# Cross-attention stage: turn of normed rows ahead of the first weighted sums, and four steps moved on ScalarE, GpSimd and VectorE

## The chip, the cores and the metric

The kernel runs on one NeuronCore of a Trainium2 chip. Its engines run unsynchronised, each with a queue of its own, and meet only at semaphores: TensorE (PE, with its weight loads shown apart as PEld), VectorE (DVE), ScalarE (ACT), GpSimd (POOL) and SyncE (SP), which here only issues DMAs. The metric is the device time of the whole program in microseconds, as the median of several runs.

## The reference

A decoder layer on 64 sequences of 64 tokens, width 256, all in float32: self-attention with 32 heads, cross-attention, and a mixture of 8 experts with one shared expert. The change touches only the stage of the middle one. Cut to what matters:

```python
x = x + attn(layernorm(x))                       # self-attention, 32 heads of 64, 8 KV heads, sinks, RoPE
x = x + xattn(layernorm(x), ctx, ctx)            # 8 heads that split the TOKENS: 8 tokens each, m = n = 256
x = x + ffn(layernorm(x))                        # top-1 of 8 experts, and a shared expert

def xattn(q, k, v):                              # b = 64, d = c = 64, m = n = 256
    qh, kh, vh = (a.reshape(b * 8, 8, 256) for a in (q, k, v))
    qk = einsum('bdm,bdn->bmn', qh, kh) / sqrt(8)
    sm = softmax(qk, axis=-1)
    return einsum('bmn,bcn->bcm', sm, vh).reshape(b, c, m)

def ffn(x):
    logits = x @ router_w.T                      # 8 experts
    # the best one, its sigmoid score scales the row that goes to it
```

## The kernel before, in words

Self-attention (`attention`) runs first and leaves, for each tile of 128 tokens (two sequences), the operands of the cross-attention in DRAM, stacked in 96 rows. Then `cross` runs over NT = 32 tiles with 16 heads each, and `experts` follows.

`cross` is a software pipeline in which each engine has its own `body(tile, one, two, three, four, five)`. In the body of `tile` the engine works on five tiles at once: `tile` itself (stage one), the one before it `w` (two), `v` two before it (three), `z` three before it (four) and `y` four before it (five). `tiles` peels the first 4 tiles, loops over 24 in steps of 4, and peels the rest. A body has STEPS = 8 steps r = 0 to 7. The order of the calls in a body is the order in the engine's queue, and a call that waits for a semaphore holds all that is behind it in that queue. Nothing but these written orders sets the schedule.

What each engine does for a body:

- TensorE, at every step: half of a pair of transposed score blocks (`turned_scores_x`, L1288, two matmuls each into one of two banks of bankXT, each may start when ScalarE's exp has read what stood there), four score matmuls for two heads (`scores_x`, L1276, into two of four banks of bankX), and the other half of the pair. From step 4 on the turned scores are those of `w`, up to step 3 those of `v`. The first turned scores of a tile, at step 4, wait for the rows 96 and 97 of stq, which carry the negated maxima (the shift of the softmax) and come by DMA. Beside these: `turn_max` at step 1 (turns the maxima of `w` into bankM), `results_x(v, 0)` at step 1 and `results_x(v, 1)` at step 5 (the weighted sums of `v`, 32 column-tiled instructions each, into bankN), `turn_norm` at step 2 (turns the normed rows of `y` into bankM), `logits` at step 3, `rank` behind the second sums at step 5, `turn_ctx` at step 7.
- VectorE: `max_x` (L1190) at every step, a reduction over the two heads that `scores_x` left; `invert(z)` at step 0 (reciprocal of the denominators, L1204), `normalise(y)` at step 1 (L1218), `choose(y)` at step 4, `place(y)` ahead of the maxima of step 6 (it waits for `rank`), `stats_of(z)` at step 7.
- ScalarE: two exps of 128 x 512 at every step (`exp_x`, L1143), and ahead of them `evac_ctx` at step 0, `evac_shift` (L1112) at 2, `evac_norm` (L1124) at 3, `exp_score` (L1129) at 5, `evac_sums` (copies bankN into nd, L1117) at 6, `scale_row` (L1136) at 7.
- GpSimd: `quotient(z)` (three operations, L1027, L1030, L1033), `weigh(y)` (1 / (1 + exp(-score)), L1046 to L1050), `send(y)` (the indirect DMA of the routed rows), `split_max(tile)`, `spread(z)`.
- SyncE, in this order: the inverses out (waits for `invert`), the shifts into stq (L956), the inverses in (L915), x2 out, the context and the stacked operands of the next tile (L898, L903), x1 in, the denominators (L976, L977, wait for `evac_sums`), the normed rows out.

Of the kernel before, what the change touches and what calls it, by code (L numbers as in the profile page):

```python
# [98 lines left out]
def need(eng, sem, value):  # L99

    if isinstance(value, int) and value <= 0:
        return
    eng.wait_ge(sem, value)
# [679 lines left out]
def cross(nc, A, G, NT, NRT):  # L783
# [6 lines left out]
    with ExitStack() as pb:  # L790
# [66 lines left out]
        def prev(tile, n):  # L857

            k = tile[1] - n
            return tile[0] + k // U, k % U  # L860

        def at(tile):
            return tile[0] * U + tile[1]

        def inside(tile):
            return not isinstance(at(tile), int)
# [121 lines left out]
        def _(pool):  # L988
# [54 lines left out]
            def weigh(y):  # L1043

                pool.wait_ge(c_fin, at(y) + 1)
                need(pool, s_xr3, at(y))  # L1046
                settle(y, 2)
                nc.gpsimd.tensor_scalar(score[:, 1:2], score[:, 0:1], 1.0, None, ALU.add).then_inc(g_sc, 1)
                pool.wait_ge(g_sc, at(y) + 1)
                nc.gpsimd.tensor_tensor(score[:, 2:3], score[:, 1:2], minus[:], ALU.pow).then_inc(s_esc, 1)  # L1050
# [19 lines left out]

            def body(tile, one, two, three, four, five):
                z, y = prev(tile, 3), prev(tile, 4)
                if four:
                    quotient(z)
                if five:
                    weigh(y)
                    send(y)
                if one:
                    split_max(tile)
                if four:  # L1080
                    spread(z)
                if not inside(tile) and 1 <= at(tile) < 4:
                    split_shared(at(tile) - 1)
# [13 lines left out]
        @block.scalar  # L1097
        def _(act):
            def evac_ctx(w):
                act.wait_ge(s_cTp, at(w) + 1)  # L1100
                need(act, s_xp, (at(w) - 1) * 2)
                if isinstance(at(w), int) and at(w) == 0:
                    act.wait_ge(s_zc, 2)
                nc.scalar.activation(cT[w[1] % 2][:, :, :, 0:XD],
                                     bM[:, 0, 0:D].rearrange("p (k h c) -> p k h c", k=2, c=XD),
                                     ACT.Copy).then_inc(s_cT, 1)

            def evac_shift(w):
                act.wait_ge(s_shp, at(w) + 1)
                r = prev(w, 2)  # L1110
                need(act, s_sh[r[1]], (r[0] + 1) * 32)
                nc.scalar.activation(sh[w[1] % 2][:], bM[0:32, 0, D:2 * D], ACT.Copy).then_inc(s_shv, 1)  # L1112

            def evac_sums(v):
                act.wait_ge(s_xp, (at(v) + 1) * 2)
                need(act, s_num, at(v) - 1)
                nc.scalar.activation(nd[v[1] % 2][:], bN[:, 0, :].rearrange("p (k m) -> p k m", k=2),  # L1117
                                     ACT.Copy).then_inc(s_nd, 1)

            def evac_norm(y):  # L1120
                act.wait_ge(s_f3p, at(y) + 1)
                o = prev(y, 1)
                need(act, s_fst[o[1] % 2], (pair(o) + 1) * 32)
                nc.scalar.activation(xn3T[:], bM[:, 0, 0:D].rearrange("p (k n) -> p k n", k=2),  # L1124
                                     ACT.Copy).then_inc(s_f3, 1)

            def exp_score(y):
                act.wait_ge(s_top, at(y) + 1)
                nc.scalar.activation(score[:, 0:1], top8[:, 0:1], ACT.Exp, scale=-1.0).then_inc(c_fin, 1)  # L1129

            def scale_row(y):

                yp = y[1] % 2
                act.wait_ge(s_esc, at(y) + 1)
                need(act, s_scat[yp], pair(y) * 16)
                nc.scalar.activation(xr[yp][:, 0:D], xn3[yp][:], ACT.Copy, scale=score[:, 2:3]).then_inc(s_xr3, 1)  # L1136

            def exp_x(w, q):
                head = at(w) * XH + q
                act.wait_ge(s_xst, head + 1)  # L1140
                if q % 8 == 0:
                    need(act, s_xp, at(w) * 2 + q // 8 - 1)
                nc.scalar.activation(xe[q][:].rearrange("p n m -> p (n m)"), bT[:, q % 2, :],  # L1143
                                     ACT.Exp).then_inc(s_xe, 1)

            def body(tile, one, two, three, four, five):
                w, v, z, y = prev(tile, 1), prev(tile, 2), prev(tile, 3), prev(tile, 4)
                for r in range(STEPS):
                    if three and r == 0:
                        evac_ctx(v)  # L1150
                    if two and r == 2:
                        evac_shift(w)
                    if five and r == 3:
                        evac_norm(y)
                    if five and r == 5:
                        exp_score(y)
                    if three and r == 6:
                        evac_sums(v)
                    if five and r == 7:
                        scale_row(y)  # L1160
                    if two and r >= LAG:
                        exp_x(w, 2 * (r - LAG))
                        exp_x(w, 2 * (r - LAG) + 1)
                    if three and r < LAG:
                        exp_x(v, 2 * (r + STEPS - LAG))
                        exp_x(v, 2 * (r + STEPS - LAG) + 1)

            def high_x(g):
                act.wait_ge(G.s_xin[g % 2], 16 * (g // 2 + 1))
                need(act, G.s_u, FF // P * (g - 1))  # L1170
                nc.scalar.activation(G.xsh[g % 2][:], G.xs[g % 2], ACT.Copy).then_inc(G.s_xs0, 1)

            def ahead_of(t):
                if t == NT + 1:
                    high_x(0)

            G.act = evac_norm, exp_score, scale_row, high_x
            tiles(act, body, ahead_of)

        @block.vector  # L1180
        def _(dve):
# [63 lines left out]
            def body(tile, one, two, three, four, five):  # L1245
                z, y = prev(tile, 3), prev(tile, 4)
                routing = Chain(dve, c_rt, 4, at(y))
                for r in range(STEPS):
                    if five and r == 6:
                        place(y, routing)  # L1250
                    if one:
                        max_x(tile, r)
                    if four and r == 0:
                        invert(z)
                    if five and r == 1:
                        normalise(y)
                    if five and r == 4:
                        choose(y, routing)
                    if four and r == 7:
                        stats_of(z)  # L1260
# [9 lines left out]
        def _(pe):  # L1270
# [54 lines left out]
            def turn_norm(y, two):  # L1325
                pe.wait_ge(s_norm, at(y) + 1)
                pe.wait_ge(s_shv, at(y) + 4 if two else NT)
                for i in range(2):
                    ins = turn(bM[:, 0, i * P:(i + 1) * P], xn3[y[1] % 2][:, i * P:(i + 1) * P])
                ins.then_inc(s_f3p, 1)  # L1330
# [20 lines left out]
            def body(tile, one, two, three, four, five):  # L1351
                w, v, y = prev(tile, 1), prev(tile, 2), prev(tile, 4)
                for r in range(STEPS):
                    if two and r >= LAG:
                        turned_scores_x(w, 2 * (r - LAG))
                    if three and r < LAG:
                        turned_scores_x(v, 2 * (r + STEPS - LAG))
                    if one:
                        scores_x(tile, r)
                    if two and r >= LAG:  # L1360
                        turned_scores_x(w, 2 * (r - LAG) + 1)
                    if three and r < LAG:
                        turned_scores_x(v, 2 * (r + STEPS - LAG) + 1)
                    if two and r == 1:
                        turn_max(w)
                    if three and r == 1:
                        results_x(v, 0)
                    if three and r == 5:
                        results_x(v, 1)
                    if five and r == 2:  # L1370
                        turn_norm(y, two)
                    if five and r == 3:
                        logits(y)
                    if five and r == 5:
                        rank(y)
                    if two and r == 7:
                        turn_ctx(w)
# [614 lines left out]
```

## Time and profile before

| | |
|---|---|
| time, median of 3 runs | 1825.08 us (1822.34 to 1825.66) |
| the profiled execution, its own time | 1829.2 us |
| its span | 1827.2 us |
| busy: TensorE, weight loads | 1724.7 us (94%), 1385.0 us (76%) |
| busy: VectorE, ScalarE, GpSimd | 1184.1 us (65%), 816.4 us (45%), 838.5 us (46%) |
| first and last copy of sums (L1117) in the cross stage | 964.8 us, 1423.1 us, 32 of them |

The page counts an engine as busy while one of its instructions runs; matmuls are pipelined and their ends are modelled, so that a busy TensorE is not one at its peak. The cross stage is the stretch from about 930 to 1423 us. In it, one tile follows another about every 14.7 us.

### The profile page before, as it was taken

Reading aid. Unit: us, or ns where it says so; the run is one execution under the profiler, and the core shown is the slowest. Engines: PE = TensorE matmul, PEld = TensorE weight load, DVE = VectorE, ACT = ScalarE, POOL = GpSimd, SP = SyncE. Lnnn points to the kernel's source line nnn. Section 1 sums busy time; section 2 is a strip of 40 time slices with the busy share of each in tenths; the row PEclk is TensorE's granted clock in tenths of the full one; section 3 lists DMA queues with packets and bytes.
Section 4 is the critical chain, followed back from the end, with each engine's and each line's share of the span. In section 5 each row is a group of like instructions: output and inputs, shape, how many; then the busy total and the mean of one; then the engine's idle time right before and its main releaser. Section 6 shows DMA issues by size and latency. Waiting matters only on the chain. (4 is left out here: it accounts for less than half of the span.)

```text
span 1827.2 us, 45302 instructions
## 1 busy us (share of the span) xinstructions
PE 1724.7 (94%) x15345; PEld 1385.0 (76%) x15441; DVE 1184.1 (65%) x2269; ACT 816.4 (45%) x1579; POOL 838.5 (46%) x1302
## 2 busy tenths in 40 slices
PE   3999999999999999999869999999999899999997
PEld 2788888888888888888757777777776899766664
DVE  5777777777777777777668788788886454322221
ACT  3434334334334334334317777777777534211111
POOL 4455555555555555554443444444444331144443
PEclk9999999999999999999879999999999999999999
DMA  5021121121121121121233444444443366322221
GB/s 186 19 59 41 47 57 41 45 57 43 43 57 43 43 57 43 43 57 39 61 90 100 121 122 124 119 121 120 119 119 93 97 187 229 105 65 66 69 63 36
DMA packets 145343, 148.43 MB, mean 81 GB/s; under 512 B 26194, under 2 KB 139926, under 8 KB 143482
## 3 DMA queue, kind: packets, MB, share of 16 engines
q1 hardware_dynamic: 138362, 120.87, 24.3%
q0 software_dynamic: 5760, 14.06, 2.4%
q10 hardware_dynamic: 1152, 12.58, 2.2%
q8 instruction: 43, 0.70, 0.2%
q14 instruction: 26, 0.21, 0.0%
HBM read 93.46 MB, written 54.11 MB: 81 GB/s over the span
## 5 line engine op out<-in xcount | busy, mean ns | idle before, releaser
L1195 DVE TENSOR_REDUCE xmax<-bankX 128x4 f32<-128x1024 f32 x256 | 308.9, 1217 | 63.7 <-PE bankX L1284 58.8
L1143 ACT ACTIVATE xe<-bankXT 128x512 f32<-128x512 f32 x512 | 292.0, 598 | 93.6 <-PE bankXT L1295 79.4
L1295 PE MATMUL bankXT<-stq,stk 98*128 98x256 f32 x1024 | 229.5, 310 | 11.9 <-ACT xe L1143 5.4
L369 POOL TENSOR_TENSOR roped<-ropeC,ropeD 128x512 f32<-128x512 f32 x160 | 205.1, 1289 | 57.0 <-DVE ropeD L530 57.0
L1295 PEld LDWEIGHTS bankXT<-stq,stk 98*128 98x128 f32 x1024 | 156.0, 191 | 55.3 <-ACT xe L1143 36.1
L557 DVE TENSOR_TENSOR oTl<-bankV,oTh 128x512 fp32r<-128x512 f32 x128 | 88.2, 689 | 166.8 <-ACT oTh L445 166.8
L662 PE MATMUL bankQ<-wqh,xnTh 128*128 128x512 f32 x384 | 188.9, 492 | 0.0
L1284 PE MATMUL bankX<-stk,stq 96*128 96x256 f32 x1024 | 171.4, 292 | 14.8 <-DMA rw<-in_rw 10.9
L361 POOL TENSOR_TENSOR prob<-prob,rden 128x1024 f32<-128x1024 f32 x64 | 121.9, 1904 | 88.9 <-DVE rden L553 88.9
L1284 PEld LDWEIGHTS bankX<-stk,stq 96*128 96x128 f32 x1024 | 145.1, 196 | 18.8 <-DMA rw<-in_rw 11.1
L1800 PE MATMUL bankX<-wexp,xT 128*128 x320 | 152.1, 599 | 2.3 <-DVE xT L1666 2.3
L728 PE MATMUL bankO<-woh,oTh 128*128 128x256 f32 x512 | 152.5, 298 | 0.0
L662 PE MATMUL bankQ<-wql,xnTh 128*128 128x512 f32 x384 | 152.2, 396 | 0.0
L662 PE MATMUL bankQ<-wqh,xnTl 128*128 128x512 f32 x384 | 152.1, 396 | 0.0
L713 PE MATMUL bankV<-probT,vbd 128*128 128x256 f32 x512 | 136.8, 390 | 9.8 <-ACT probT L439 9.8
L728 PE MATMUL bankO<-wol,oTh 128*128 128x256 f32 x512 | 143.4, 280 | 0.0
L728 PE MATMUL bankO<-woh,oTl 128*128 128x256 f32 x512 | 143.3, 280 | 0.0
L527 DVE TENSOR_TENSOR ropeC<-bankQ,const 128x512 f32<-128x512 f32 x160 | 109.5, 684 | 40.5 <-PE bankQ L662 40.5
L1310 PE MATMUL bankN<-xe,cT 128*32 128x256 f32 x2048 | 125.5, 386 | 0.4 <-ACT xe L1143 0.4
L439 ACT ACTIVATE probT<-bankP 128x512 f32<-128x512 f32 x128 | 76.2, 595 | 109.0 <-PE bankP L639 109.0
L445 ACT ACTIVATE oTh<-bankV 128x512 fp32r<-128x512 f32 x128 | 76.5, 598 | 103.6 <-PE bankV L713 103.6
L1027 POOL TENSOR_TENSOR xpart<-nd,xrden 128x512 f32<-128x512 f32 x32 | 41.1, 1283 | 174.6 <-DMA xrden<-inv_d 174.6
(189 smaller groups left out, 3884.9 us busy)
## 6 DMA issues: line engine op xcount, KB each, us to landing
stackk_d<-chl SPq DMA_DIRECT2D x96, 128.0 KB, 2.3
stackq_d<-q2hl SPq DMA_DIRECT2D x96, 128.0 KB, 2.3
stk<-stackk_d SPq DMA_DIRECT2D x32, 384.0 KB
stq<-stackq_d SPq DMA_DIRECT2D x128, 96.0 KB
wexp<-in_wexp ACTq DMA_DIRECT2D x8, 1536.0 KB, 8.3
x_d<-x SPq DMA_DIRECT2D x64, 128.0 KB, 1.9
xrden<-inv_d SPq DMA_DIRECT2D x64, 128.0 KB, 2.5
xin<-xg_d SPq DMA_DIRECT2D x40, 128.5 KB, 2.1
```

Source lines behind the costliest of these rows:

```text
L361: nc.gpsimd.tensor_tensor(v, v, rden[:, r, :].unsqueeze(2).to_broadcast([P, 16, HD]), ALU.mult).then_inc(s_pn, 1)
L369: nc.gpsimd.tensor_tensor(roped[c % 3][:], ropeC[c % 2][:], ropeD[c % 2][:], ALU.add).then_inc(s_rsum, 1)
L527: nc.vector.tensor_tensor(ropeC[c % 2][:].rearrange("p (h d) -> p h d", d=HD), src.rearrange("p (h d) -> p h d", d=HD), cos.unsqueeze(1).t ...
L662: ins = nc.tensor.matmul(out, a[p][:, k, :], w[:, k, col:col + 512], start=False, stop=(k == 1 and n == 2))
L713: ins = nc.tensor.matmul(out[:, :, b, :], vbd[u[1]][b][:, g, :], src[:, :, b, :], start=True, stop=True)
L728: ins = nc.tensor.matmul(out, a[g % 2][:, j, :], w[:, 4 * g + j, :], start=False, stop=(g == 3 and j == 3 and n == 2))
L1143: nc.scalar.activation(xe[q][:].rearrange("p n m -> p (n m)"), bT[:, q % 2, :], ACT.Exp).then_inc(s_xe, 1)
L1195: nc.vector.tensor_reduce(xmax[tile[1] % 2][:, :, a:b + 1:b - a].rearrange("p m h -> p h m"), bS[:, 2 * (pr % 2):2 * (pr % 2) + 2, :].rear ...
L1284: ins = nc.tensor.matmul(bS[:, q % 4, m * D:(m + 1) * D], stq[p][0:96, hd, m * P:(m + 1) * P], stk[p][0:96, hd // 4, :], start=True, stop= ...
L1295: ins = nc.tensor.matmul(bT[:, q % 2, n * D:(n + 1) * D], stk[p][0:98, hd // 4, n * P:(n + 1) * P], stq[p][0:98, hd, :], start=True, stop= ...
L1310: ins = nc.tensor.matmul(bN[32 * j:32 * j + 32, 0, (m % 2) * D:(m % 2 + 1) * D], c[:, k, 160 * j + 32 * m:160 * j + 32 * m + 32], xe[4 * b ...
L1800: ins = nc.tensor.matmul(out, xT[p][:, k, :], weights(base, (k * 2 + half) * FF, FF), start=(k == 0), stop=(k == 1))
```

## The change

Five edits, all of order, none of what is computed.

- GpSimd: `weigh(y)` runs ahead of `quotient(z)`, where it ran behind it.
- ScalarE: `scale_row(y)` at step 6 and `evac_sums(v)` at step 7, where the sums were copied at step 6 and the row scaled at step 7.
- VectorE: `invert(z)` at step 1, behind the maxima of that step and ahead of `normalise(y)`, where it stood between the maxima of step 0 and of step 1.
- TensorE: `results_x(v, 0)` at step 2 behind `turn_norm(y)`, where it stood at step 1, ahead of the scores of step 2.

```diff
 # gpsimd body
                 z, y = prev(tile, 3), prev(tile, 4)
+                if five:
+                    weigh(y)
                 if four:
                     quotient(z)
                 if five:
-                    weigh(y)
                     send(y)
 # scalar body
                     if five and r == 5:
                         exp_score(y)
-                    if three and r == 6:
+                    if five and r == 6:
+                        scale_row(y)
+                    if three and r == 7:
                         evac_sums(v)
-                    if five and r == 7:
-                        scale_row(y)
 # vector body
                     if one:
                         max_x(tile, r)
-                    if four and r == 0:
+                    if four and r == 1:
                         invert(z)
                     if five and r == 1:
                         normalise(y)
 # tensor body
                     if two and r == 1:
                         turn_max(w)
-                    if three and r == 1:
+                    if five and r == 2:
+                        turn_norm(y, two)
+                    if three and r == 2:
                         results_x(v, 0)
                     if three and r == 5:
                         results_x(v, 1)
-                    if five and r == 2:
-                        turn_norm(y, two)
```

## Rows read from the trace of the kernel before

**Rows 1.** Busy time by engine over 100 us of the cross stage: us, engines, PEclk, DMA.
```profile
1100.00:1200.00 100.00, 97.71 (x953) 77.26 (x955) 81.90 (x173) 72.42 (x151) 41.80 (x86) 1.00 0.45 116
```

**Rows 2.** Chain of waits, cross stage 1000 to 1420 us: total, times, longest us.
```profile
PEld bankXT L1295 <- ACT xe L1143: 32.3, 119, 0.8
```

**Rows 3.** Timeline, TensorE's weight loads of one tile: start, us, instruction, idle before.
```profile
1127.98 0.30 PEld L1295 LDWEIGHTS bankXT<-stq,stk 98*128 98x128 f32 x2
...
1133.02 0.15 PEld L1274 LDWEIGHTS bankM<-const,xhl 128*32 128x32 f32 x2
...
1133.39 1.45 PEld L1310 LDWEIGHTS bankN<-xe,cT 128*32 128x32 f32 x32 [0.21 <-ACT xe L1143]
...
1135.25 0.30 PEld L1295 LDWEIGHTS bankXT<-stq,stk 98*128 98x128 f32 x2 [0.41 <-issue]
...
1136.21 0.25 PEld L1274 LDWEIGHTS bankM<-const,xn 128*128 128x128 f32 x2
...
1136.44 0.30 PEld L1295 LDWEIGHTS bankXT<-stq,stk 98*128 98x128 f32 x2
...
1137.92 0.30 PEld L1295 LDWEIGHTS bankXT<-stq,stk 98*128 98x128 f32 x2
...
1142.65 0.30 PEld L1295 LDWEIGHTS bankXT<-stq,stk 98*128 98x128 f32 x2
```

**Rows 4.** The same timeline and tile, VectorE alone.
```profile
1128.19 0.17 DVE L1238 TENSOR_TENSOR pos<-bankM,run 128x8 f32<-128x8 f32 x1 [0.18 <-PE bankM L1341]
...
1131.99 1.23 DVE L1195 TENSOR_REDUCE xmax<-bankX 128x4 f32<-128x1024 f32 x1
...
1133.13 0.34 DVE L1204 RECIPROCAL xiden<-xden 128x32 f32<-128x32 f32 x1
...
1134.47 0.40 DVE L1218 TENSOR_SCALAR xn<-x,mvb,rstdb 128x256 f32<-128x256 f32 x1
```

**Rows 5.** The same timeline and tile, ScalarE alone.
```profile
1127.68 0.60 ACT L1117 ACTIVATE nd<-bankN 128x512 f32<-128x512 f32 x1 [0.87 <-PE bankN L1310]
...
1129.74 0.50 ACT L1136 ACTIVATE xr<-xn,score 128x256 f32<-128x256 f32 x1
...
1131.36 2.51 ACT L1143 ACTIVATE xe<-bankXT 128x512 f32<-128x512 f32 x4
```

**Rows 6.** The same timeline, the SP queue's DMA issues.
```profile
1133.50 1.28 SPq L908 DMA_DIRECT2D inv_d<-xiden  x2
...
1134.83 1.20 SPq L956 DMA_DIRECT2D stq<-sh  x2
```

**Rows 7.** The line that moves the shifts to stq (L956), 1000 to 1400 us.
```profile
DMA to landing us min/median/max: 2.1/2.1/2.6
```

**Rows 8.** Timeline of TensorE's weight loads at 1346 us: a late shift row.
```profile
1345.99 0.30 PEld L1295 LDWEIGHTS bankXT<-stq,stk 98*128 98x128 f32 x2 [0.77 <-DMA stq<-sh]
```

**Rows 9.** Timeline of TensorE at 1027 us: a late load of the next tile.
```profile
1027.19 0.73 PE L1284 MATMUL bankX<-stk,stq 96*128 96x256 f32 x4 [0.42 <-DMA stq<-stackq_d]
```

**Rows 10.** The timeline of Rows 3, VectorE, ScalarE and POOL around the routing.
```profile
1124.76 1.29 POOL L1027 TENSOR_TENSOR xpart<-nd,xrden 128x512 f32<-128x512 f32 x1 [5.34 <-DMA xrden<-inv_d]
...
1125.63 0.20 ACT L1129 ACTIVATE score<-top 128x1 f32<-128x1 f32 x1 [0.52 <-DVE top L1226]
...
1126.10 0.78 DVE L1231 TENSOR_SCALAR onehot<-const,idxf 128x8 f32<-128x8 f32 x1
1126.12 0.73 POOL L1030 TENSOR_TENSOR xwhole<-xa,xpart 128x256 f32<-128x256 f32 x1
...
1127.00 0.73 POOL L1033 TENSOR_TENSOR x<-xwhole,xpart 128x256 f32<-128x256 f32 x1
...
1128.25 0.57 POOL L1050 TENSOR_TENSOR score<-score,minusb 128x1 f32<-128x1 f32 x1
...
1128.39 0.17 DVE L1239 CUSTOM_DVE_ANT_0 ptmp<-pos,onehot 128x8 f32<-128x8 f32 x1
...
1140.78 0.23 DVE L1231 TENSOR_SCALAR onehot<-const,idxf 128x8 f32<-128x8 f32 x1
```

## The prediction

> **What bounds the kernel now.** I began with busy time by stretches, to see which engine the cross stage hangs on. TensorE is busy 97.7 of 100 us at a granted clock of 1.00, VectorE 81.9, ScalarE 72.4 [rows 1]. So no engine but TensorE is full on average, and a gain can only come from its few gaps. The chain of waits says what the gaps are: the weight loads of the turned scores wait for ScalarE's exps, 32.3 us in 420 us [rows 2]. At 14.67 us for a tile (1127.98 to 1142.65 [rows 3]) that is 28.6 tiles and 1.13 us in each. Nothing else in that view held TensorE as long, so this is the most that a new order can give back. Then I laid one tile out in order of time, engine by engine, since the change is one of order. All times below are of that tile. Its landmarks on TensorE: 1127.98 first turned scores of step 6, 1133.02 `turn_max`, 1133.39 first weighted sums, 1135.25 step 2, 1136.21 `turn_norm`, 1136.44 step 3, 1137.92 step 4, 1142.65 the next tile's step 6 [rows 3].
>
> **TensorE: the sums behind the turn of the normed rows.** Nothing is added to its work: the same 0.96 us of step 2 (1135.25 to 1136.21), 0.23 us of `turn_norm` and 1.86 us of sums (1133.39 to 1135.25) are put in another order [rows 3]. What matters is when each is ready.
>
> Step 2 can't start at once behind `turn_max`. Its first turned scores wait for the third of four exps that run 1131.36 to 1133.87, 0.63 us each [rows 5], so for 1133.25; with 0.1 us from the exchange on ScalarE (below) 1133.35. Plus 0.96 us, TensorE stands at `turn_norm` at 1134.3.
>
> `turn_norm` needs the normed rows of VectorE. Those end at 1134.47 + 0.40 = 1134.87 [rows 4]. Now this is hidden by 1.34 us (1136.21 less 1134.87), and the cover is just the sums that are moved away. VectorE can't be earlier: from `place` at 1128.19, which itself waits for `rank` on TensorE, to the norm it goes from one instruction to the next, with eight instructions of maxima, statistics and reciprocal between that close up on each other; its ends are shown [rows 4]. Putting `invert` behind the maxima of step 1 changes the order in that string and not its length.
>
> So: norm 1134.87, about 0.08 us to wake TensorE (estimate, between 0.03, the gap from the reciprocal's end 1133.47 to the SP issue at 1133.50 [rows 4, 6], and about 0.1), turn 1134.95, weights 0.25 us, the idle 0.21 us that stands ahead of the sums now, sums from 1135.41, and 1.86 us on, step 3 at 1137.27. Today it is 1136.44 [rows 3]. That is 0.83 us a tile, of which 0.65 us is new waiting for VectorE and the rest is the wait for the third exp and the idle time that now stands behind a wider weight load.
>
> From step 3 on all of it is as before. Step 4 begins 1.48 us later (1136.44 to 1137.92), sums, `rank` and the next step 6 another 4.73 us later (1137.92 to 1142.65) [rows 3]. That stretch includes one wait for an exp, which the change doesn't touch: the exp of step 4 starts when its scores are there. `rank` shifts by the whole 0.83 us, so `place` does, and with it the string on VectorE: a closed loop, and so the 0.83 us is paid at each tile and isn't made up.
>
> **ScalarE: row at step 6, sums at step 7.** The copy of sums waits 0.87 us for TensorE and ends at 1128.28, the row takes 0.50 us at 1129.74 between exps [rows 5]. Exchanged, the row falls into the idle 0.87 us and the copy between exps: 0.60 for 0.50 us, 0.1 us later for all exps up to step 2. This is in the 1134.3 above and hidden by the wait for the norm. The row finds its score only because `weigh` comes early. The copy `evac_norm` (ahead of the exps of step 3) now lies under the moved sums, where ScalarE has nothing to do anyway. It gives nothing to TensorE, as the exps behind it need turned scores that come behind the sums.
>
> The copy of sums ends some 2.0 us later (1130.34 for 1128.28), and so do the denominators. Their two DMA issues follow it and `invert` has till 1134.2, 3.9 us, so it doesn't wait for them; `results_x` of the next tile needs bankN free only 5 us later.
>
> **VectorE and SP: the inverse at step 1.** `invert` moves from 1133.13 to behind the maxima, about 1134.21, and ends 1134.55 instead of 1133.47: 1.08 us later. Behind it in the SP queue stand all of its DMAs: inverses out, the shifts, the inverses in, x2, the context and the next tile's operands. The inverses out would go from 1133.50 to 1134.58 and the shifts from 1134.83 to 1135.91, the second half 0.6 us on, at 1136.51 [rows 6]. With 2.1 us to land [rows 7] they are there at 1138.6. Today they land at 1137.5 and step 4, which needs them, starts at 1137.92: 0.4 us of margin. With step 4 put off by the 0.83 us to 1138.75, 0.15 us is left. So the delay of the shifts and that of the norm run beside each other and don't add: the shifts alone would cost 0.7 us. That one such row can hold TensorE is seen at 1345.99, 0.77 us [rows 8]. Landing spreads up to 2.6 us [rows 7], which bounds this at 0.35 us a tile more.
>
> The next tile's operands leave 1.08 us later too and are needed 0.83 us later, so they lose 0.25 us of margin. At 1027.19 they already come 0.42 us too late [rows 9]; such places stand at the back edge of the loop, six times. 6 x 0.25 = 1.5 us.
>
> **GpSimd: `weigh` first.** It waits for ScalarE's score (ends 1125.83), and the quotient, now at 1124.76, waits behind it. `weigh` took 1.09 us (from the quotient's end 1127.73 to 1128.82), so the quotient starts near 1126.95 and ends 3.0 us later, 2.2 us later than now [rows 10]. Who waits for it: the statistics at about 1131.35, ahead of the maxima at 1131.99 [rows 4], so x2 at 1129.95 is in time. `send` and `split_max` stand behind it and end no later than now, since `send` today waits for the row.
>
> **Sum.** The bodies in which all five stages run are those of tiles 4 to 31: 28. 28 x 0.83 = 23.2 us, with 1.5 us of loads 24.7 us. The profiled execution took 1829.2 us, 4.1 us over the median of the runs shown; so 1854 us for it and 1825.1 + 24.7 = 1850 us as the median. Bounds of the likeliest case: below, 0.55 us a tile if VectorE's string ends 0.3 us earlier, 1840 us; above, 0.83 + 0.35 us, 1860 us.
>
> **Rivals.**
>
> *VectorE and GpSimd collide (slower still).* With `weigh` first, the quotient's second operation starts 1.36 us behind its first (1124.76 to 1126.12), so near 1128.3 and lasts 0.73 us. It meets `place`, whose product of positions (L1239, two inputs in SBUF) starts at 1128.39. The row of `onehot` shows what that can cost: 0.78 us beside that operation at 1126.10, 0.23 us alone at 1140.78 [rows 10]. Behind `rank`, a block of up to 0.7 us goes into VectorE's closed loop: 28 x 0.7 = 20 us more, 1870 us. For it: both start within 0.1 us of each other by this sum. Against: whoever is first wins, and the product took 0.17 us beside the power operation [rows 10]. The Trainium skill ("SBUF — State Buffer", Who interferes with whom) says that a VectorE instruction with two SBUF inputs contends with a GpSimd one that reads SBUF, and that the second to issue blocks fully; the `onehot` row agrees in size, though not in kind, since it has one tensor input. By that rule alone I would expect the upper sum. I take none of it, as the order is open.
>
> *Faster.* TensorE's waits for exps are dissolved by the new places of row, sums and norm copy. It decides if the normed rows are there by 1134.3, that is if VectorE's string ends 0.6 us earlier. All 1.13 us gone would be 32 us; half is the more that a moved copy of 0.4 to 0.5 us can do: 28 x 0.55 = 15 us, 1810 us. For: ScalarE's idle time (0.87 us) is indeed filled. Against: the copy of sums filled it already, and ten exps instead of eight now stand ahead of the first sums.
>
> *No difference.* VectorE early and the shifts early by their margins: waits only change places, 1825 us, within 3 us.
>
> **How the numbers follow.** Likeliest 0.60 (1840 to 1860), collision or late loads 0.18 (1860 to 1874), faster 0.15 (1796 to 1821), no difference 0.07. The range 1824 to 1872 takes in the first, most of the second and half of the last, a little over 8 in 10. A run can tell 0.2%, 3.7 us, from no change: slower 0.79, the same 0.06, faster 0.15.
>
> **What would show it.** Right: a new wait of TensorE's `turn_norm` (L1274, xn) for VectorE of 0.6 us in 28 tiles; tiles 15.5 us apart; shifts landing within 0.2 us of step 4, in some tiles late; the copy of sums without its 0.87 us. Collision: L1239 near 0.9 us, tiles over 16 us apart. Wrong: no wait ahead of `turn_norm`, and waits for exps under 0.7 us a tile. The norm's end is the number on which all hangs.

## The result

| | before | after |
|---|---|---|
| median | 1825.37 us (1822.34 to 1827.94) | 1864.12 us (1861.48 to 1864.91) |
| ratio | | 1.0212, 95% interval 1.0197 to 1.0227 |
| the profiled execution, its span | 1829.2 us, 1827.2 us | 1864.91 us, 1862.9 us |
| first and last copy of sums in the cross stage | 964.8, 1423.1 us | 966.6, 1466.7 us |

The changed kernel is 38.8 us slower, against the 25 us of the forecast; 1864 us lies inside its range. From the first to the last copy of sums it takes 500.1 us for 458.3 us, 41.8 us more, so all of the loss lies in the cross stage. Behind the last copy the profiled execution of after is 7.9 us shorter (396.2 for 404.1 us). The profiled execution of before lay 3.8 us above its median; where it lost them, and what the rest of the 7.9 us is, wasn't looked into.

The chain of waits of the changed kernel, 1000 to 1440 us (engine, line waited for, releaser: total us, times, longest). Line numbers above 1075 are one up on those of before.

```profile
PEld bankXT L1296 <- ACT xe L1144: 32.3, 111, 0.8
...
PE bankM L1275 <- DVE xn L1219: 16.9, 27, 0.7
...
PE bankXT L1296 <- DMA stq<-sh: 3.2, 9, 0.9
```

Two waits of TensorE are new beside those of [rows 2]: the turn of the normed rows (L1275) for the norm, and step 4's turned scores for the DMA of the shifts, in some tiles by this view; the medians of all tiles in the part on why the prediction was right show that every tile pays. The waits for exps, 32.3 us in the 420 us of [rows 2], are 32.3 us in 440 us here: the new order gave none of them back. The copy of sums no longer waits for TensorE.

One tile of the changed kernel in order of time, all engines, cut to the landmarks of [rows 3 to 6, 10]:

```profile
1130.72 0.30 PEld L1296 LDWEIGHTS bankXT<-stq,stk 98*128 98x128 f32 x2
...
1131.12 0.74 POOL L1030 TENSOR_TENSOR xwhole<-xa,xpart 128x256 f32<-128x256 f32 x1
1131.22 0.66 DVE L1240 CUSTOM_DVE_ANT_0 ptmp<-pos,onehot 128x8 f32<-128x8 f32 x1
...
1132.47 0.59 ACT L1118 ACTIVATE nd<-bankN 128x512 f32<-128x512 f32 x1
...
1136.84 0.31 PEld L1296 LDWEIGHTS bankXT<-stq,stk 98*128 98x128 f32 x2
...
1137.37 0.34 DVE L1205 RECIPROCAL xiden<-xden 128x32 f32<-128x32 f32 x1
1137.63 0.31 DVE L1219 TENSOR_SCALAR xn<-x,mvb,rstdb 128x256 f32<-128x256 f32 x1
1137.74 1.27 SPq L908 DMA_DIRECT2D inv_d<-xiden  x2
...
1138.07 0.20 PEld L1275 LDWEIGHTS bankM<-const,xn 128*128 128x128 f32 x2 [0.92 <-issue]
...
1138.44 1.45 PEld L1311 LDWEIGHTS bankN<-xe,cT 128*32 128x32 f32 x32 [0.17 <-issue]
...
1139.06 1.21 SPq L956 DMA_DIRECT2D stq<-sh  x2
1140.31 0.30 PEld L1296 LDWEIGHTS bankXT<-stq,stk 98*128 98x128 f32 x2 [0.41 <-issue]
...
1141.98 0.30 PEld L1296 LDWEIGHTS bankXT<-stq,stk 98*128 98x128 f32 x2 [0.20 <-issue]
...
1146.70 0.30 PEld L1296 LDWEIGHTS bankXT<-stq,stk 98*128 98x128 f32 x2
```

From step 6 (1130.72) to the next step 6 (1146.70) it is 15.98 us for 14.67 us [rows 3]. The last turned scores of step 2 are loaded from 1136.84, and some 0.25 us later TensorE could load for the turn. It waits for the norm instead, which ends at 1137.94, and the turn starts at 1138.07. The product of positions (L1240) starts 0.10 us behind GpSimd's second quotient operation (1131.12) and takes 0.66 us; it ends as that ends. That is the usual case, as min, median and max of that line say, before (L1239) and after:

```profile
L1239 DVE CUSTOM_DVE_ANT_0 ptmp<-pos,onehot x32: 166/167/199, 994.1 to 1461.3; 128x8 f32<-128x8 f32 x32
```
```profile
L1240 DVE CUSTOM_DVE_ANT_0 ptmp<-pos,onehot x32: 166/628/754, 1000.5 to 1502.1; 128x8 f32<-128x8 f32 x32
```

### The profile page after: what moved, and what is told of

It is laid out like the page before. It is cut to its first block and busy times, and to the rows that moved or that the text cites. A ratio compares the mean times of both kernels' runs of the same rounds, so it can differ in the third digit from the quotient of the medians.

```text
span 1862.9 us, 45403 instructions
## 1 busy us (share of the span) xinstructions
PE 1741.8 (93%) x15440; PEld 1388.6 (75%) x15441; DVE 1182.9 (63%) x2269; ACT 821.3 (44%) x1579; POOL 840.6 (45%) x1302
## 5 line engine op out<-in xcount | busy, mean ns | idle before, releaser
L1311 PE MATMUL bankN<-xe,cT 128*32 128x256 f32 x2048 | 131.5, 400 | 0.6 <-ACT xe L1144 0.6
L329 POOL TENSOR_TENSOR spare_g<-half_neg 128x1 f32<-128x1 f32 x130 | 25.3, 195 | 204.0 <-DVE mv L499 199.5
```

Of the source, the lines that this page charges most:

```text
L1311: ins = nc.tensor.matmul(bN[32 * j:32 * j + 32, 0, (m % 2) * D:(m % 2 + 1) * D], c[:, k, 160 * j + 32 * m:160 * j + 32 * m + 32], xe[4 * b ...
```

## The experiments

Each ratio is against the kernel before, run on the same chip beside it. Its median there is given where microseconds are compared.

### TensorE's edit alone

Edit: only the order of `turn_norm` and `results_x(v, 0)` at step 2, in the kernel before.

> The kernel before with the TensorE edit alone: first weighted sums at step 2 behind the turn of the normed rows; GpSimd, ScalarE and VectorE as before. Theory A (TensorE waits for VectorE's normed rows, which the sums used to cover): 0.83 us a tile in 28 tiles, 23 us, 1848 us, and a wait of the turn for the norm of about 0.6 us. Rival B (the loss of the changed kernel comes from GpSimd's quotient, which now collides with the product of positions on VectorE): nothing of that is in here, so within 5 us of before, 1825 to 1830 us. Rival C (the inverses, now a step later, push the shifts back in the SP queue): also not in here, 1825 to 1830 us.

Measured: 1849.1 us for 1828.8 us, ratio 1.0118 (1.0101 to 1.0135), 21.5 us. Its chain of waits, 1000 to 1420 us:

```profile
PE bankM L1274 <- DVE xn L1218: 15.6, 28, 0.8
```

The wait for the norm stands there in 28 cases and 15.6 us. This one edit carries over half of the loss, at the predicted size (23 us), and neither a collision on VectorE nor the place of the inverse can explain it, since this kernel has neither: its product of positions (L1239) takes 0.167 us in the median, as before, and its inverse stands at step 0.

### VectorE's edit alone

Edit: only the inverse, in the kernel before.

```diff
-                    if four and r == 0:
+                    if four and r == 1:
                         invert(z)
```

> The kernel before with invert at step 1 alone. Theory A alone (VectorE's normed rows bound the tile): the order of the inverse and the maxima leaves the norm where it is, and the sums still cover it, so 1825 us. Rival C (shifts pushed back by 1.08 us in the SP queue with 0.39 us of margin): 0.69 us a tile, 19 us, 1844 us, with waits of TensorE at step 4 for the DMA into stq in most tiles. I hold both mechanisms for real, in parallel in the changed kernel, and expect 1844 us here.

Measured: 1894.7 us, ratio 1.0355 (1.0338 to 1.0373): 65 us where I expected at most 19 us, and more than all edits together cost. The chain of waits, and busy time by microsecond in one tile (us, TensorE, weight loads, VectorE, ScalarE, GpSimd, then the granted clock, DMA share, GB/s):

```profile
PE bankXT L1295 <- DMA stq<-sh: 22.2, 24, 1.3
```
```profile
1126.00:1127.00 1.00, 0.81 (x8) 0.72 (x6) 1.00 (x2) 1.00 (x3) 0.00 (x0) 1.00 0.07 16
1127.00:1128.00 1.00, 0.00 (x0) 0.00 (x0) 0.45 (x1) 0.13 (x1) 0.00 (x0) 1.00 0.08 23
1128.00:1129.00 1.00, 0.93 (x7) 0.94 (x8) 0.00 (x0) 0.31 (x1) 0.00 (x0) 1.00 0.68 212
1129.00:1130.00 1.00, 0.94 (x6) 0.74 (x5) 0.92 (x1) 0.89 (x2) 0.22 (x1) 0.60 0.67 194
...
1131.00:1132.00 1.00, 1.00 (x10) 0.52 (x13) 1.00 (x2) 0.67 (x2) 0.78 (x2) 0.50 0.82 266
...
1139.00:1140.00 1.00, 1.00 (x9) 1.00 (x9) 0.83 (x1) 0.77 (x2) 0.22 (x1) 0.78 0.00 0
```

The shifts do come late, in 24 waits and by 22.2 us, 0.93 us each, which is one in nearly every tile. That is the expected mechanism. What I had not expected stands in the column of the clock: TensorE is idle from 1126.7 to 1128.1, once, and from 1129.4 to 1139.5 it is granted 0.50 of its clock, the lower of its two levels. The sums of step 5 show the price. The 32 instructions of such a half take 1.86 us to the next step at the full clock [rows 3]; here:

```profile
1131.35 3.64 PE L1310 MATMUL bankN<-xe,cT 128*32 128x256 f32 x32
...
1134.92 0.50 PEld L1340 LDWEIGHTS bankM<-onehot,const 128*128 128x128 f32 x2 [0.81 <-issue]
```

It is 3.57 us from 1131.35 to `rank` at 1134.92. Over 400 us of the stage the mean granted clock is 0.89 here and 1.00 before:

```profile
1000.00:1400.00 400.00, 372.60 (x3253) 283.43 (x3252) 272.51 (x597) 246.33 (x502) 146.43 (x299) 0.89 0.38 102
```

The tile shown is an extreme one. Looked at in steps of 0.25 us, the clock falls 19 times in these 400 us; most of the low stretches are about a third as long as this one, and behind a few of the waits it doesn't fall at all. The typical tile, by the medians over 1000 to 1420 us, takes 2.43 us from step 3 to step 4 for 1.49 us before, which is the wait, and 6.29 us from step 4 to the next step 6 for 4.72 us before, where no new wait of that size stands: 0.94 and 1.57 us. The second part I put down to the clock. So one late DMA of 0.9 us costs 65 us / 28 = 2.3 us a tile. The Trainium skill ("TensorE: Matmul & The Clock Gate", What's actually happening) describes two states, 1.2 and 2.4 GHz; the trace agrees in the two levels, 0.50 and 1.00 of the clock.

### The product of positions without its second input in SBUF

Edit: the changed kernel, with pos8 in a free strip of bankM.

```diff
-                ch(nc.vector.tensor_tensor(pos8[:], bM[:, 0, D + 8:D + 16], run[:], ALU.add))
+                ch(nc.vector.tensor_tensor(bM[:, 0, D + 24:D + 32], bM[:, 0, D + 8:D + 16], run[:], ALU.add))
...
-                    in0=pos8[:], in1=onehot[:]
+                    in0=bM[:, 0, D + 24:D + 32], in1=onehot[:]
```

> The changed kernel, with the sum of rank and running count (pos8) written to a free strip of bankM in PSUM instead of SBUF, so that the product of positions (L1240) reads one tensor from SBUF and one from PSUM; nothing else moves. Rival B (the product blocked by GpSimd's second quotient operation, 0.63 us for 0.17 us, lengthens VectorE's string in each tile): the product falls back to about 0.2 us, 0.46 us a tile in 28 tiles, 13 us less, 1851 us. If the string is not the bound in the changed kernel, or if the later inverse holds all: 1864 us as the changed kernel. If it is the two inputs in SBUF that matter, the product must shrink; if it is any VectorE operation beside GpSimd, it stays at 0.63 us.

Measured: 1861.1 us for 1828.8 us, ratio 1.0174 (1.0157 to 1.0191). Against 1.0212 of the changed kernel that is 0.4%, 7 us, with intervals that just don't meet. The line, and its place in one tile:

```profile
L1240 DVE CUSTOM_DVE_ANT_0 ptmp<-bankM,onehot x32: 166/166/167, 1000.8 to 1495.4; 128x8 f32<-128x8 f32 x32
```
```profile
1129.98 0.30 PEld L1296 LDWEIGHTS bankXT<-stq,stk 98*128 98x128 f32 x2
...
1130.36 0.74 POOL L1030 TENSOR_TENSOR xwhole<-xa,xpart 128x256 f32<-128x256 f32 x1
1130.49 0.17 DVE L1240 CUSTOM_DVE_ANT_0 ptmp<-bankM,onehot 128x8 f32<-128x8 f32 x1
...
1138.01 1.21 SPq L956 DMA_DIRECT2D stq<-sh  x2
1139.25 0.30 PEld L1296 LDWEIGHTS bankXT<-stq,stk 98*128 98x128 f32 x2 [0.41 <-issue]
...
1140.93 0.30 PEld L1296 LDWEIGHTS bankXT<-stq,stk 98*128 98x128 f32 x2 [0.21 <-issue]
```

The product runs beside the same GpSimd operation (1130.36 to 1131.10) in 0.17 us in all 32 tiles. So what blocked it was its two inputs in SBUF, not the company of GpSimd as such. The rule of the Trainium skill ("SBUF — State Buffer", Who interferes with whom) that the forecast cited and took nothing of agrees with both numbers: two inputs in SBUF, a block; one, none. By that rule the product should also have been blocked in the kernel before, where it starts 0.14 us behind GpSimd's power operation and yet takes 0.17 us [rows 10]; between 990 and 1430 us it starts under that operation in 16 of 30 tiles and never takes over 0.2 us; the profile's spans on GpSimd are rough, and this stays open. Of the 0.46 us, 0.32 us reach TensorE in the two tiles shown: step 6 to step 3 is 9.27 us here (1129.98 to 1139.25) and 9.59 us in the changed kernel. Over all tiles of 1000 to 1420 us the medians are 9.32 and 9.58 us, so 0.26 us. Where the rest is taken up wasn't looked into.

### The changed kernel with the old place of the sums

Edit: `results_x(v, 0)` back at step 1, all else as changed.

> The changed kernel with the TensorE edit alone undone: first weighted sums back at step 1. Theory A alone: all is given back, 1825 to 1830 us. Theory C beside it: the sums cover the norm again, but the inverse still ends 1.08 us later and, with the product blocked by 0.46 us ahead of it in VectorE's string, 1.5 us later; less the margin of 0.39 us it is 1.15 us a tile, 32 us, 1857 us, all of it as waits of step 4 for the DMA into stq. I expect 1855 us.

Measured: 1889.1 us, ratio 1.0333 (1.0315 to 1.0351). Undoing the edit that costs 21 us alone makes the changed kernel 22 us slower (1.0333 for 1.0212). The wait for the shifts is there as expected:

```profile
PE bankXT L1296 <- DMA stq<-sh: 23.1, 24, 1.9
```

23.1 us in 24 tiles; the mean clock over the stage is 0.91. I had expected 1.15 us of wait a tile, near the 0.96 us here, and priced it without the clock, so 1855 us was 34 us too low.

### The sums at step 2, but ahead of the turn

Edit: the changed kernel with `results_x(v, 0)` and `turn_norm(y, two)` of step 2 exchanged.

> The changed kernel with the first weighted sums still at step 2, but ahead of the turn of the normed rows. Theory A alone: the wait of 0.72 us for the norm lies under the sums again, 20 us less, 1845 us. Theory C beside it: VectorE's string and the SP queue stay as they are, the shifts land at the same time, so step 4 starts no earlier and TensorE waits there for 1.1 us in one piece instead of 0.7 and 0.2 us in two; the tile stays at 16.0 us, and if one piece of over 1 us costs the clock as in the run of invert only, 1885 us. I expect 1880 us, slower than the changed kernel.

Measured: 1889.9 us, ratio 1.0348 (1.0319 to 1.0378). The waits, and the same row by stretches as above for 1000 to 1400 us, this kernel's and the changed kernel's:

```profile
PE bankXT L1296 <- DMA stq<-sh: 24.1, 25, 1.4
```
```profile
1000.00:1400.00 400.00, 369.47 (x3332) 282.07 (x3332) 279.89 (x607) 252.43 (x516) 148.60 (x306) 0.92 0.40 103
```
```profile
1000.00:1400.00 400.00, 370.47 (x3504) 286.07 (x3504) 299.98 (x638) 269.52 (x544) 157.74 (x319) 0.99 0.41 108
```

The norm is covered again, and what it saves comes back at step 4 as one wait, 24.1 us in 25 tiles, and with it the clock falls to 0.92. The changed kernel waits about as long per tile, but in two pieces of some 0.7 and 0.3 us, and keeps 0.99. The two kernels differ in nothing but the order of two calls, so it is how the idle time is cut and where it lies, and not its sum, that goes with the clock. In the changed kernel the shifts' delay therefore hides behind the norm's, as the forecast said, and the two delays together are worth less than the second alone.

### The changed kernel with the old place of the inverse

Edit: `invert(z)` back at step 0, all else as changed.

> The changed kernel with invert back at step 0. If the later inverse were simply a loss (theory C alone): the shifts are early again, 0.2 us a tile less, 1858 us. But the sums are copied at step 7 there, their denominators land about 5.8 us after the start of step 6, and VectorE reaches step 0's inverse at 5.1 us: it would wait 0.6 us there, ahead of the maxima of step 1 and of the norm for which TensorE waits, 17 us more, 1880 us. I expect 1875 us and a wait of the reciprocal for the denominators in most tiles.

Measured: 1864.3 us, ratio 1.0185 (1.0153 to 1.0218), not to be told from the changed kernel. The waits:

```profile
PE bankM L1275 <- DVE xn L1219: 25.7, 26, 1.6
...
DVE xiden L1205 <- DMA xden<-nd: 5.6, 12, 0.8
```

The reciprocal waits for the denominators in 12 of 26 tiles and 5.6 us, not in most and not 0.6 us each. TensorE's waits for the norm are longer, 25.7 us in 26 for 16.9 us in 27, by more than these 5.6 us; the rest wasn't looked into. By the medians of the tiles, step 6 to step 3 is 9.80 us for 9.58 us and step 3 to step 4 is 1.39 us for 1.68 us: what the earlier shifts give is spent on the later norm. The step to 1 was a fair companion of copying the sums at step 7, but no gain; my 1875 us took the landing to be later than it is.

### Shifts first in the SP queue

Edit: the inverse at step 1 in the kernel before, and on SP: shifts, inverses out, x2, context, stk, inverses in, stq.

> The kernel with invert at step 1 alone, as in the run of invert only, and the SP queue in another order: shifts into stq first, then inverses out, x2, context, the next tile's stk, inverses in, the next tile's stq. Theory C (the later inverse costs only because the shifts stand behind it in the SP queue, and TensorE's long wait at step 4 then costs its clock for some 10 us in each tile): the shifts leave at 1134.15 of the tile shown for before, the wait at step 4 and the clock loss go together, 1825 to 1835 us for 1895 us. Rival D (the later inverse itself, by way of the quotient, x2 and the statistics, holds the tile): no change, 1890 us or more. The next tile's stq leaves 0.3 us later than before, which may cost up to 5 us.

Measured: 1948.3 us, ratio 1.0636 (1.0588 to 1.0684). The shifts never hold TensorE here. Others do:

```profile
POOL xpart L1034 <- DMA xrden<-inv_d: 228.9, 21, 12.0
...
PE bankXT L1302 <- ACT xe L1150: 64.5, 22, 4.4
ACT xr L1143 <- POOL score L1057: 58.8, 22, 4.1
```

The new SP order issues the inverses in some 2.7 us later behind `turn_max` (5.9 us for 3.2 us). The quotient waits for them, `weigh` stands behind it on GpSimd in this kernel, the row on ScalarE waits for `weigh` (58.8 us in 22 tiles) with all exps behind it, and TensorE stands up to 4.4 us. The mean granted clock over 1000 to 1400 us is 0.85. So this run doesn't decide whether a late inverse costs by itself or by what stands behind it: my edit made a chain of its own. It does show what the GpSimd edit protects from.

### The same candidate order with the row at step 6

Edit: the kernel before with weigh first, `scale_row` and then `evac_sums` at step 6, pos8 in PSUM, and the SP order of the run above.

> A candidate built on the kernel before: weigh first on GpSimd; ScalarE scales the row at step 6 ahead of the copy of sums, both at step 6; pos8 in PSUM; the SP queue with the shifts first (as in the run of the inverse at step 1 with shifts first); sums and inverse where they were before. The row falls into the 0.87 us in which ScalarE waits for the second sums, the copy stays where it was, and 0.4 us goes out of ScalarE's string ahead of the first sums. If TensorE's waits for exps there are what I take them for, 0.3 to 0.4 us a tile, 10 us faster than before, ratio 0.994 to 0.996. If the next tile's operands come late or another wait takes their place: within 3 us of before.

Measured: 1841.2 us for 1828.6 us, ratio 1.0068 (1.0044 to 1.0092), 0.7% slower where I expected up to 0.6% faster. The timeline shows the late quotient again, now by another way:

```profile
1122.24 0.73 PE L1292 MATMUL bankX<-stk,stq 96*128 96x256 f32 x4 [0.29 <-DMA stq<-stackq_d]
...
1123.15 0.43 DVE L1217 BATCH_NORM_STATS2 statsb<-x 128x6 f32<-128x256 f32 x1 [0.65 <-POOL x L1040]
...
1125.19 0.11 PEld L1282 LDWEIGHTS bankM<-const,xhl 128*32 128x32 f32 x2 [0.99 <-POOL xhl L1027]
```

VectorE's statistics wait 0.65 us for x2, `turn_max` waits 0.99 us for GpSimd's split of the maxima, and the next tile's stq lands late. The waits of TensorE for that split are 18.3 us in 21 cases over 1000 to 1420 us. What the earlier shifts and the row gave was lost to the inverses in, which this order puts late in the SP queue.

### A late inverse with nothing behind it

Edit: the inverse at step 1 in the kernel before, weigh first, pos8 in PSUM; the shifts are issued by ScalarE, and on SP x2 and context go ahead of the inverses in.

```diff
 # scalar, end of evac_shift
+                act.wait_ge(s_shv, at(w) + 1)
+                for part in range(2):
+                    nc.scalar.dma_start(stq[w[1]][96 + part:97 + part].bitcast(F32),
+                                        sh[w[1] % 2][part * XH:(part + 1) * XH, :].bitcast(F32)).then_inc(s_sh[w[1]], 16)
 # sync body
-                if two: ...                      # the shifts
-                if four:
-                    inverses_in(z)
                 if five:
                     store_x2(y)
                 if one:
                     ...                          # context
+                if four:
+                    inverses_in(z)
+                if one:
                     ...                          # next tile
```

> The kernel before with invert at step 1, and what makes a later inverse expensive taken out of its way: the two DMAs of the shifts are issued from ScalarE's queue behind evac_shift, where ScalarE waits 1.67 us anyway, x2 and the context stand ahead of the inverses in on SP so that the next tile's operands leave as before, weigh stands first on GpSimd so that a late quotient can't hold ScalarE's row, and pos8 is in PSUM. Theory C (a late inverse costs by what is queued behind it, first the shifts): 1828 to 1834 us for 1895 us of the inverse alone, and no wait of step 4 for the DMA into stq. Rival D (the late inverse costs by itself, through the quotient and the statistics): over 1850 us.

Measured: 1824.8 us for 1826.9 us, ratio 0.999 (0.9974 to 1.0006). With the inverse at the same late place the 65 us are gone, and so is every wait for the shifts. The inverse costs nothing that can be measured by being late itself, only by what is queued behind it. The cures went in together, so this run doesn't say how much each of them is worth; the trace of the inverse alone names the shifts as the one new wait of TensorE.

### The changed kernel with the same cures

Edit: the changed kernel with pos8 in PSUM, the shifts by ScalarE, x2 and context ahead of the inverses in. It still has the exchange on ScalarE and the inverse at step 1.

> The changed kernel with pos8 in PSUM, the shifts issued from ScalarE's queue, and x2 and context ahead of the inverses in: the product's block and the wait of step 4 are taken out, the wait of TensorE for the norm stays. If the norm's wait is the rest of the loss: 0.83 us a tile, 23 us, 1850 us, the same as the kernel before with the TensorE edit alone. If there is a fourth cause: over 1857 us.

Measured: 1847.8 us for 1826.9 us, ratio 1.011 (1.0083 to 1.0137), the same as TensorE's edit alone, 1.0118. Its waits of TensorE for the norm are 13.5 us in 27 tiles, and none is left for the shifts:

```profile
PE bankM L1274 <- DVE xn L1218: 13.5, 27, 0.7
```

There is no fourth cause of a size that can be measured (the interval is 5 us to either side).

### GpSimd's edit alone

Edit: `weigh(y)` ahead of `quotient(z)` in the kernel before.

> The kernel before with the GpSimd edit alone: weigh ahead of the quotient. The quotient's second operation meets the product of positions on VectorE, which should take 0.63 us for 0.17 us as in the changed kernel. Theory B with cover: the norm has 1.34 us of cover and pays nothing, but the inverse at step 0 ends 0.3 us later, and the shifts behind it have some 0.17 us of margin by the trace of the changed kernel with pos8 in PSUM (2.9 us from the first issue to the start of step 4): 0.1 us a tile, 4 us, ratio 1.001 to 1.004. Without any such chain: 1.000. If the product isn't lengthened here, the block belongs to the changed kernel's own phase of the engines.

Measured: 1828.6 us for 1826.1 us, ratio 1.0009 (0.9992 to 1.0025). The product is blocked here too, and the shifts are late in a few tiles:

```profile
L1240 DVE CUSTOM_DVE_ANT_0 ptmp<-pos,onehot x32: 166/598/754, 995.5 to 1462.5; 128x8 f32<-128x8 f32 x32
```
```profile
PE bankXT L1296 <- DMA stq<-sh: 2.3, 8, 0.7
```

The same block of 0.43 us (0.598 less 0.167) that costs 7 us in the changed kernel costs here what can't be told from nothing, since the sums still cover the norm. 2.3 us of waits for the shifts in 8 tiles is what comes through.

### A version that beats both

Edit: the kernel before with weigh first, the row and then the copy of sums at step 6, pos8 in PSUM, shifts by ScalarE, x2 and context ahead of the inverses in; sums at step 1 and inverse at step 0 as before.

> A candidate: the kernel before with inverse and sums where they were, weigh first, the row at step 6 ahead of the copy of sums, pos8 in PSUM, the shifts issued from ScalarE's queue, x2 and context ahead of the inverses in. The row goes into the 0.87 us in which ScalarE waits for the second sums, the shifts land some 0.6 us earlier, the next tile's operands leave no later. If the waits of TensorE for exps ahead of the first sums shrink by what the row took: 0.2 to 0.4 us a tile, 1818 to 1824 us. If VectorE's string or another wait holds the tile at 14.7 us: 1828 us.

Measured: 1815.6 us for 1826.9 us, ratio 0.9948 (0.9932 to 0.9965), 11.3 us by the medians (0.9948 of the time is 9.5 us). One tile of it:

```profile
1125.45 0.51 ACT L1136 ACTIVATE xr<-xn,score 128x256 f32<-128x256 f32 x1 [0.29 <-POOL score L1045]
...
1126.03 0.60 ACT L1117 ACTIVATE nd<-bankN 128x512 f32<-128x512 f32 x1
...
1126.33 0.30 PEld L1295 LDWEIGHTS bankXT<-stq,stk 98*128 98x128 f32 x2
...
1132.34 1.15 ACTq L1111 DMA_DIRECT2D stq<-sh  x2
...
1133.97 1.32 ACT L1143 ACTIVATE xe<-bankXT 128x512 f32<-128x512 f32 x2 [1.67 <-PE bankXT L1295]
```

The row (1125.45) and the copy (1126.03) both fit ahead of step 6's first exp, so that the 0.50 us that the row took between exps at step 7 [rows 5] is free, and the two DMA issues of 1.15 us fit into the 1.67 us in which ScalarE waits for TensorE. This was the good idea in the change: the row into ScalarE's idle time. That it needs the copy to stay where it was is argued and not shown, since in the changed kernel the wait for the norm would hide any gain. How much of the gain is the row's and how much that of pos8 and of the queues wasn't run apart; the same cures under a late inverse gave 0.999.

## Why the prediction was right in its range and 14 us short

The medians over the tiles of 1000 to 1420 us, from one landmark of [rows 3] to the next (starts of TensorE's weight loads, us), lay the runs side by side:

| kernel | step 6 to 3 | step 3 to 4 | step 4 to next 6 | tile |
|---|---|---|---|---|
| before | 8.48 | 1.49 | 4.72 | 14.68 |
| before with TensorE's edit | 9.24 | 1.39 | 4.73 | 15.36 |
| changed, with all cures | 9.24 | 1.39 | 4.73 | 15.36 |
| changed, product in PSUM | 9.32 | 1.68 | 4.73 | 15.75 |
| changed | 9.58 | 1.68 | 4.73 | 15.98 |

- **The norm behind the sums, 0.83 us a tile: right in kind, a little too large.** Step 3 begins 0.76 us later, and 0.68 us are left over the whole tile, since step 4 follows step 3 a little sooner than before (why wasn't looked into). Alone the edit costs 21.5 us for the 23.2 us of the sum, and the wait appears where it was foretold. That VectorE's string is the bound, and the sums its cover, was the number on which all hung, and it held.
- **The margin of the shifts, 0.15 us left: mis-sized.** I put the landing at 0.6 + 2.1 = 2.7 us from the first issue. In two traces step 4 starts 2.92 us behind it (1139.06 to 1141.98, 1138.01 to 1140.93). Against the kernel with all cures, whose shifts are early, step 3 to step 4 takes 0.29 us more, and in every tile (1.59 us at the least, for 1.40 us at the most), and the whole tile 0.39 us. The ratios say the same: 1.0174 with the product mended, 1.0110 with the queues mended too, 12 us. The cure also moves x2 and the context in the SP queue, so that the 0.1 us beyond the 0.29 us isn't assigned. The sum had nothing for this but an upper bound of 0.35 us; it is the larger part of what was missing.
- **The collision on VectorE, taken at nothing with a rival at 0.7 us: mis-sized.** It takes place in most tiles (median 0.628 us for 0.167 us), and I had seen both starts within 0.1 us of each other and left it out as open. It measures 0.46 us in the product and 0.23 us a tile, 28 x 0.23 = 6 us; the run with pos8 in PSUM gives 7 us. The rival was right in kind and more than double in size.
- **The sum now:** 0.68 + 0.39 + 0.23 = 1.30 us a tile, as the table has it (15.98 less 14.68); 28 tiles, 36.4 us. By the times of the runs it is 21.5, 12 and 7 us for the 38.8 us between the medians.
- **The late loads, 1.5 us in the sum:** not tried apart. The changed kernel shows such waits twice in 440 us, 0.8 us in all.
- **"The shifts alone would cost 0.7 us": wrong in the price.** The wait was 0.93 us a tile, near enough, but the kernel lost 2.3 us a tile to it, since TensorE's clock fell. That the price can be so high was in no term of the forecast. In the changed kernel the clock stays at 0.99, so the forecast for it was not hurt, by luck of the order and not by anything I had worked out.
- **ScalarE's exchange: right as far as is shown.** It wasn't run alone, but the changed kernel with all cures contains it and costs the same as TensorE's edit alone. The forecast that the copy of sums loses its wait and the row needs `weigh` early held too. What I missed is that the row's idle place could be had without moving the copy, which together with the cures of the queues is worth some 10 us.
- **The faster and the neutral rival fell:** waits for exps are as long as before.

## What to carry to other kernels

Before work is moved away from between a producer and its consumer, ask what it covers: here 1.86 us of sums let the norm be ready 1.34 us before it was needed, and moved behind it they covered nothing of its way. When a producer moves later, read on in every queue that waits for it: the inverse itself cost nothing, and what stood behind it in the SP queue, the two small DMAs of the shifts first of all, cost 65 us with the clock that fell. And let an engine's idle time be filled by what is already ready, without pushing out what used to fill it.

## What the runs showed of the hardware

- Behind one idle stretch of TensorE of about 1.3 us in each tile its granted clock fell from 1.00 to 0.50 in most tiles, for 10 us in the one shown and for about a third of that in most, 0.89 in the mean of 400 us. Waits of 22 us in sum went with a loss of 65 us. Two shorter idle stretches, 0.7 and 0.3 us, in tiles of the same kind left the mean at 0.99.
- A VectorE product with both inputs in SBUF took 0.66 us beside a GpSimd addition and ended with it; beside a GpSimd power operation of one element a partition it took 0.17 us. With one input in PSUM it took 0.17 us beside the same addition, in 32 of 32 tiles.
- The DMAs of the shifts issued from ScalarE's queue landed in 2.2 us (median), from SP's in 2.1 us, and took 1.15 us of its queue for two.
